# An MoE kernel on one core: dispatched rows turned by transposing DMAs in place of TensorE

## What is computed

```python
gates = softmax(x_flat @ gating_w)                   # 1024 tokens, 8 experts
topk_w, topk_idx = top_k(gates, 2)
norm_w = topk_w / sum(topk_w)
capacity = ceil(1024 * 2 / 8 * 1.25)                 # 320 slots for each expert
position = (running count of earlier picks of the same expert)
buf[expert, position] = x_flat[token]                # picks past 320 are dropped
h = relu(einsum('ecd,edh->ech', buf, w1) + b1)       # w1: 8 x 256 x 1024
out_e = einsum('ech,ehd->ecd', h, w2) + b2           # w2: 8 x 1024 x 256
out[token] += norm_w * out_e[expert, position]
```

## Time and profile before

| | us |
|---|---|
| three executions | 528.79, 537.62, 538.77 (median 537.62) |
| profiled execution | 532.26 |
| its span | 530.4 |
| TensorE busy | 453.4 |
| DVE busy | 383.9 |
| ScalarE busy | 277.2 |
| GpSimd busy | 234.2 |
| mean granted TensorE clock | 0.96 of full |

### The profile page before, as it was taken

One profiled execution on the slowest core, in us unless ns is written; L12 is line 12 of the kernel. 1 busy time (PEld: TensorE's weight loads), 2 busy tenths in 40 slices (PEclk: granted clock), 3 DMA queues, 4 the chain that ended last, 5 costly groups with the idle time before them and its releaser, 6 DMA issues. The chain is left out here.

```text
span 530.4 us, 11842 instructions
## 1 busy us (share of the span) xinstructions
PE 453.4 (85%) x4579; PEld 337.8 (64%) x4586; DVE 383.9 (72%) x873; ACT 277.2 (52%) x612; POOL 234.2 (44%) x301
## 2 busy tenths in 40 slices
PE   4964977898979999898998998897757999999984
PEld 3442544336857777787776776685534777777753
DVE  4479474767677888887886786886558588887881
ACT  2667556566355666554655454555215355556630
POOL 3275031101422222433554255433338377787764
PEclk9986699999999999999998999999978999999998
DMA  8991001930170000000060001000103666677632
GB/s 277 268 331 18 0 2 27 380 135 1 40 239 4 1 1 1 3 2 1 1 223 22 1 1 43 22 2 7 42 12 102 212 149 167 143 196 205 177 37 30
DMA packets 37720, 46.74 MB, mean 88 GB/s; under 512 B 7584, under 2 KB 33056, under 8 KB 37472
## 3 DMA queue, kind: packets, MB, share of 16 engines
q1 hardware_dynamic: 32912, 40.82, 24.1%
q0 software_dynamic: 4224, 4.79, 5.9%
q10 hardware_dynamic: 528, 0.38, 0.3%
HBM read 40.14 MB, written 8.55 MB: 92 GB/s over the span
## 5 line engine op out<-in xcount | busy, mean ns | idle before, releaser
L560 POOL TENSOR_TENSOR lw<-lw 128x512 f32<-128x512 f32 x48 | 60.7, 1269 | 113.2 <-DVE lw L1172 112.6
L868 ACT ACTIVATE lw<-psum,nmax 128x256 f32<-128x256 f32 x128 | 59.2, 469 | 19.8 <-DVE nmax L1225 19.8
L1714 PE MATMUL psum<-lp 128*128 128x256 f16 x576 | 68.4, 273 | 0.0
L1230 DVE TENSOR_TENSOR lw<-psum,lw 128x512 f16<-128x512 f32 x64 | 43.8, 684 | 28.7 <-ACT lw L875 27.7
L875 ACT ACTIVATE lw<-psum 128x512 f16<-128x512 f32 x64 | 38.2, 597 | 49.4 <-PE psum L1813 49.4
L664 POOL TENSOR_TENSOR lw<-lw 128x320 f16<-128x320 f32 x60 | 49.3, 837 | 23.0 <-DVE lw L1448 20.1
L1714 PEld LDWEIGHTS psum<-lp 128*128 128x128 f16 x576 | 54.1, 98 | 6.5 <-issue 0.5
L1976 PE MATMUL psum<-lw,se 128*128 128x320 f16 x384 | 55.2, 302 | 0.9 <-issue 0.4
L950 ACT ACTIVATE lw<-psum,b1w 128x320 f16<-128x320 f32 x64 | 33.7, 527 | 41.8 <-PE psum L1976 40.9
L1989 PE MATMUL psum<-se,lw 128*128 128x256 f16 x384 | 46.9, 281 | 7.0 <-POOL lw L664 7.0
L1813 PE MATMUL psum<-identf,lw 128*128 128x128 f32 x256 | 41.0, 283 | 13.9 <-DVE lw L1230 12.3
(11 more groups left out here) (245 smaller groups left out, 970.8 us busy)
## 6 DMA issues: line engine op xcount, KB each, us to landing
se<-in_w SPq DMA_DIRECT2D x16, 1024.0 KB, 8.0
dispatch<-in_empty SPq DMA_DIRECT2D x4, 662.5 KB, 10.1
lw<-dispatch SPq DMA_DIRECT2D x8, 265.0 KB
lp<-in_Wq SPq DMA_DIRECT2D x2, 1024.0 KB, 9.4
se<-in_WoT SPq DMA_DIRECT2D x1, 2048.0 KB, 11.8
lp<-in_w_kc_q SPq DMA_DIRECT2D x2, 768.0 KB, 9.8
x_sb<-in_x SPq DMA_DIRECT2D x2, 512.0 KB, 6.1
se<-in_gate_wT SPq DMA_DIRECT2D x1, 1024.0 KB, 9.0
```

The source lines that it names most:

```text
L560: nc.gpsimd.tensor_tensor(rope[:, c % QT, :], t1[:, c % 2, :], t2[:, c % 2, :], ALU.add)\
L868: A_(e_sb[:, n % 2, st * S:(st + 1) * S], bank[3 + n % 2][:, st * S:(st + 1) * S], ACT.Exp, bias=nmax[:, n % 2, st:st + 1], accum_out=esum ...
L1230: V.tensor_tensor(at[1][:, n % 2, :], bank[5][:, :], at[0][:, n % 2, :], ALU.subtract).then_inc(v_at, 1)
L1714: ins = M(tile_bank(c)[:, half * S:(half + 1) * S], m1[w][:, kc, half, col:col + P], (yth, ytl)[a][:, kc, b * S:(b + 1) * S], start=(n == ...
```

## The change

Rows in DRAM get 544 f16 columns (1088 bytes), so that a row starts at a multiple of 32 bytes. For experts 1 to 7 SP no longer loads whole rows: four transposing DMAs (high and low half, two blocks of 128 columns each) bring 320 rows x 128 columns each, turned, straight into one of two buffers `bufT[e % 2]`. Only the nine metadata words of a row are still loaded (three small DMAs). `turn_rows`, its copies on ScalarE and DVE and their semaphores are gone. From expert 2 on, the transposing DMAs wait until expert e-2's first product is done (`p_h`) and until all transposing DMAs of expert e-1 have landed (`d_rows`). TensorE waits for `d_rows` ahead of each expert's first product. Expert 0's rows are made as before; TensorE now waits for both halves at once (`s_bT`).

```diff
-RW = 2 * D + 2 * (1 + NE)
+META = 1 + NE
+RW = 2 * D + 32
...
-        slots_w = w3([2 * 3 * RW // 2])
+        slots_w = w3([64])[:, 0:2 * 3 * META]
...
-        bufT = w3([2, KC * CAP], F16)
+        bufT1 = w3([2, KC * CAP], F16)
+        w3([6 * 256 - KC * CAP])
+        bufT0 = w3([2, KC * CAP], F16)
+        bufT = [bufT0, bufT1]
...
                 elif e >= 2:
-                    sp.wait_ge(p_bT, 2 * (e - 1))
+                    sp.wait_ge(p_h, MH * (e - 1))
+                    sp.wait_ge(d_rows, 64 * (e - 1))
+                if e >= 1:
+                    for part in range(2):
+                        for kc in range(KC):
+                            col = part * D + kc * P
+                            sp.dma_start_transpose(bufT[e % 2][:, part, kc * CAP:(kc + 1) * CAP],
+                                                   buf_h[e * CAP:(e + 1) * CAP, col:col + P]).then_inc(d_rows, 16)
+                if e >= 2:
                     sp.wait_ge(v_meta, e - 1)
-                sp.dma_start(slots_u[:, e % 2, 0:2, :], buf_d[e * CAP:e * CAP + 2 * P, :].rearrange("(a p) c -> p a c", p=P))\
+                sp.dma_start(slots_u[:, e % 2, 0:2, :],
+                             buf_d[e * CAP:e * CAP + 2 * P, D:D + META].rearrange("(a p) c -> p a c", p=P))\
                     .then_inc(d_slot[e % 2], 16)
...
+                for j in range(2):
+                    sp.dma_start(slots_u[j * W3:(j + 1) * W3, e % 2, 2, :], buf_d[e * CAP + 2 * P:(e + 1) * CAP, D:D + META])\
+                        .then_inc(d_slot[e % 2], 16)
...
-                if e >= 1 and e + 1 < NE:
-                    rows_high(e + 1)
...
-                    rows_low(e + 1)
                     slot_meta(e + 1)
...
             for e in range(NE):
-                pe.wait_ge(a_bT, e + 1)
+                if e == 0:
+                    pe.wait_ge(s_bT, 2)
+                else:
+                    pe.wait_ge(d_rows, 64 * e)
                 pe.wait_ge(v_we, 4 * (e + 1))
...
-                                    bufT[:, a, kc * CAP:(kc + 1) * CAP], start=(k == 0), stop=(k == 5))
+                                    bufT[e % 2][:, a, kc * CAP:(kc + 1) * CAP], start=(k == 0), stop=(k == 5))
...
-                if e >= 1 and e + 1 < NE:
-                    turn_rows(e + 1)
...
-                if e == 0:
-                    turn_rows(1)
```

More of the change, by code:

```diff
@@ L207, in program @@
         w3 = carve(lw, 34)
-        slots_w = w3([2 * 3 * RW // 2])
-        slots = slots_w.bitcast(F16).rearrange("p (r i c) -> p r i c", r=2, i=3)
+        slots_w = w3([64])[:, 0:2 * 3 * META]
         slots_u = slots_w.bitcast(U32).rearrange("p (r i c) -> p r i c", r=2, i=3)
-        slots_tok = slots_u[:, :, :, D]
-        slots_wt = slots_w.rearrange("p (r i c) -> p r i c", r=2, i=3)[:, :, :, D + 1:D + 1 + NE]
-        bufT = w3([2, KC * CAP], F16)
+        slots_tok = slots_u[:, :, :, 0]
+        slots_wt = slots_w.rearrange("p (r i c) -> p r i c", r=2, i=3)[:, :, :, 1:1 + NE]
+        bufT1 = w3([2, KC * CAP], F16)
+        w3([6 * 256 - KC * CAP])
+        bufT0 = w3([2, KC * CAP], F16)
+        bufT = [bufT0, bufT1]
         hs = [w3([MH, CAP], F16) for _ in range(2)]
@@ L256, in program @@
         buf_d = nc.dram_tensor("dispatch", (SLOTS + P, RW // 2), U32).ap()
+        buf_h = buf_d.bitcast(F16)
         x_v = A["x"].rearrange("b (h p) d -> p (b h) d", p=P)
@@ L303, in program @@
         a_we, v_we = sem("a_we"), sem("v_we")
-        p_bT, a_bT, v_bT = sem("p_bT"), sem("a_bT"), sem("v_bT")
+        p_bT, s_bT, d_rows = sem("p_bT"), sem("s_bT"), sem("d_rows")
         v_hl = sem("v_hl")
@@ L427, in dispatched @@
                 elif e >= 2:
-                    sp.wait_ge(p_bT, 2 * (e - 1))
+                    sp.wait_ge(p_h, MH * (e - 1))
[7 more added lines that the diff above has]
+                if e >= 2:
                     sp.wait_ge(v_meta, e - 1)
-                sp.dma_start(slots_u[:, e % 2, 0:2, :], buf_d[e * CAP:e * CAP + 2 * P, :].rearrange("(a p) c -> p a c", p=P))\
+                sp.dma_start(slots_u[:, e % 2, 0:2, :],
+                             buf_d[e * CAP:e * CAP + 2 * P, D:D + META].rearrange("(a p) c -> p a c", p=P))\
                     .then_inc(d_slot[e % 2], 16)
-                sp.dma_start(slots_u[0:W3, e % 2, 2, :], buf_d[e * CAP + 2 * P:(e + 1) * CAP, :]).then_inc(d_slot[e % 2], 16)
-                sp.dma_start(slots_u[W3:2 * W3, e % 2, 2, D:D + 1 + NE], buf_d[e * CAP + 2 * P:(e + 1) * CAP, D:D + 1 + NE])\
-                    .then_inc(d_slot[e % 2], 16)
+                for j in range(2):
+                    sp.dma_start(slots_u[j * W3:(j + 1) * W3, e % 2, 2, :], buf_d[e * CAP + 2 * P:(e + 1) * CAP, D:D + META])\
+                        .then_inc(d_slot[e % 2], 16)
             weights(0)
@@ L931, in _ @@
             route_exp(B - 1)
[L933 to L943, removed]
+            act.wait_ge(p_bT, 1)
+            for kc in range(KC):
+                ins = A_(bufT[0][:, 0, kc * CAP:(kc + 1) * CAP], bank[SEL_BANK[0][kc]][:, 0:CAP], ACT.Copy)
+            ins.then_inc(s_bT, 1)
             for e in range(NE):
@@ L955, in _ @@
                         split_high(4 * (e + 1) + q)
-                if e == 0:
-                    rows_high(1)
         @block.vector
@@ L1420, in _ @@
             dve.wait_ge(d_b, 48)
[L1422 to L1430, removed]
+            dve.wait_ge(p_bT, 2)
+            for kc in range(KC):
+                ins = V.tensor_copy(bufT[0][:, 1, kc * CAP:(kc + 1) * CAP], bank[SEL_BANK[1][kc]][:, 0:CAP])
+            ins.then_inc(s_bT, 1)
             def slot_meta(e):
@@ L1439, in slot_meta @@
                 V.tensor_copy(tslot[:, e, 0:2], slots_tok[:, e % 2, 0:2]).then_inc(v_meta, 1)
-            rows_low(0)
             for e in range(NE):
@@ L1462, in _ @@
                     if e == 0 and i == 2:
-                        rows_low(1)
                         slot_meta(1)
@@ L1972, in _ @@
                     for a, w in PASSES:
-                        if m == 0 and a == 1:
-                            pe.wait_ge(v_bT, e + 1)
                         for kc in range(KC):
                             ins = M(bank[2 + n % 3][:, 0:CAP], we[0][w][:, e % 2, kc * EH + m * P:kc * EH + (m + 1) * P],
-                                    bufT[:, a, kc * CAP:(kc + 1) * CAP], start=(k == 0), stop=(k == 5))
+                                    bufT[e % 2][:, a, kc * CAP:(kc + 1) * CAP], start=(k == 0), stop=(k == 5))
                             k += 1
                     ins.then_inc(p_h, 1)
-                if e >= 1 and e + 1 < NE:
-                    turn_rows(e + 1)
                 if e >= 1:
```

## The result

| | before | changed |
|---|---|---|
| median of 20 runs each, us | 537.44 (525.23 to 544.46) | 543.50 (531.13 to 549.83) |
| profiled execution, us | 532.26 | 538.58 |
| its span | 530.4 | 536.8 |
| ratio | | 1.0139, 95% interval 1.0072 to 1.0207 |

The account below looks back on a forecast made before the run. Bound: TensorE's 14.8 us per expert and a nearly equal loop of landing and splitting through one raw buffer. Start gains 0.5 us, steady part nothing: 535.0 - 0.5 = 534.5 us, own range 529 to 539, widened for rivals to 526 to 560.

Parts of the forecast that it names:

- the loop of landing and splitting: Experts 3 to 6: load, landing and splits through one raw buffer take 15.42, 15.46 and 29.47 us for two; TensorE's cycle 14.8.
- the 7.8 us of turns: TensorE: six turns of 1.30 us ahead of expert 6's first product, at most 7.8 us on the path to the end.
- the 6 us forecast: Expert 1: its transposes land at 409.8, TensorE needs them at 415.77, so hidden with 6 us to spare.
- the forecast landing, 7.7 us: Expert 1's transposes: small loads end at 403.7, landing 6.1 us later at 409.8; SP's release was at 402.13.
- Rival 1: Between weight landings: transposes fill the DMA ring; 10.7 us for four gives +21 us, 555 us; chance 0.36.
- the sum: Whole kernel: 532.26 us profiled minus 0.5 gives 531.8; forecast set at 535.0 - 0.5 = 534.5 us.
- Issue 409.8 to 413.4, small loads 1.6, weights at 415.0 instead of 412.48.: SP's queue at expert 2: its transposes and small loads go first, so its weights leave at 415.0, not 412.48.
- The term of 0.9 us per transposing DMA: SP's issue time: 0.9 us each, 3.6 us for an expert's four, within a range of 1.5 to 6.6 us.
- So they are hidden and the loop stays.: Experts 3 to 6: transposes of 6.1 us fit in 7.7 us, leaving the loop at 60.35 us.
- the ring's free time: Between one expert's weights landing and the next's first byte: 5.75 us of splitting plus some 2 us, 7.7 us.
- TensorE's idle 1.5 us per expert costs clock: TensorE, expert processing: full clock expected at 13.5 of 15 us busy; if not, +2 to +8 us; chance 0.04.
- at nothing: Expert 0's start: waiting for both halves of its rows costs nothing, under 1 us exposed at worst.

## Why the prediction was wrong

Right, by its own steps: the bound was read rightly. TensorE was not alone on the path, the loop of landing and splitting was; the 7.8 us of turns brought nothing there, and the version with a second raw buffer shows them coming in once that loop is gone. The transposes stayed hidden from TensorE, with less to spare at expert 1 than the 6 us forecast: the DMA traffic of its four transposes ends at about 404.7, 7.6 us after the release, and TensorE began at 9.9. That the forecast landing, 7.7 us, fits so well is luck: the issue was taken 1.5 us too short and the rest as much too long. Rival 1's mechanism, a ring filled by movement, did not come: 2.0 us per engine, not 10.7. The median, 543.5 us, lies inside the stated range of 526 to 560, but the range was widened upwards for that rival, so this is no merit of the sum.

Wrong, and the sign with it:

1. "Issue 409.8 to 413.4, small loads 1.6, weights at 415.0 instead of 412.48." From the release that is 12.9 us; measured 17.1. The term of 0.9 us per transposing DMA was 1.25, which over the eight that stand ahead is 2.8 us. And I took the second four to start when the first had landed, at 7.7 us, and left out that SP itself was still busy: expert 1's small loads and the store of x (403.88 to 407.26) came first, so they started at 10.2 us. The landing was not the wait that ended last; SP's own list was.
2. "So they are hidden and the loop stays." I checked the transposes against the ring's free time and not against SP's. Expert 4's and expert 6's weights went out 0.9 and 0.3 us after DVE was ready, and landed 10.8 to 10.9 us after issue, against 8.1 to 9.6 us in the kernels that kept the transposes behind them. Against 9.7 that is 1.9 and 1.5 us. Why they landed later is open: the plain DMAs stood ahead of them in the same way (8.6 to 9.5 us), and so did twice the transposes (8.4 to 9.4 us).
3. The rival that "TensorE's idle 1.5 us per expert costs clock" had a chance of 0.04, since the waits were forecast even and short. They were uneven, 3.3 to 8.7 us at every second expert, and the products behind them took 1.9, 2.6 and 1.5 us more. Short waits did cost no clock, as said; the forecast of their length failed.
4. Expert 0's wait for both halves was put "at nothing". It moved DVE's splits to where less of GpSimd's work runs beside them, and expert 1 started 5.0 us earlier than before instead of the 1.3 us of its turn. Item 1 lost this again and more: expert 2 started 3.4 us later than before.

The end therefore came 11.4 us later in this pair, where the sum said 0.5 us earlier: SP's issue (items 1 and 2) made the waits, and the products behind them (item 3) took 6.0 us more than before, likely by the clock.

## What to carry to other kernels

Price an added DMA on the queue that issues it before pricing its movement, and walk the issuing engine's whole list, small loads and stores too, to where the critical transfer stands. In an in-order queue the transfer that is needed last goes last: tiny loads that an engine reads first, then the one that closes the tightest loop, then the expensive and patient ones. Work taken off the busiest engine shortens the period only when no other loop, here one raw buffer, has the same period; give that loop its second buffer first.

## What the runs showed of the hardware

- A transposing DMA of 320 x 128 two-byte elements held SP for 1.25 us (median of 28; 1.12 to 2.12), a plain one of as many bytes for 0.43 us (0.32 to 2.08); its movement took at most 0.5 us on each of the 16 engines. The Trainium skill (VectorE: DVE Perf Modes, The three transpose paths) gives 1309 ns for one block of 128 x 128. An estimate from the page's figure for four of these DMAs, ten such blocks, is 13 us; from the first issue to the end of their traffic they took some 6.0 us (398.71 to 404.7), 5.1 of them issue. The measurement decides.
- Of the first products of experts 2 to 6, those behind waits of 0.4 to 1.9 us took 6.7 to 6.9 us, as those without a wait; those behind waits of 2.2 us and more took 8.0 to 9.4 us, where the clock was read (0.77 and 0.71) a part of them at the lower level, with one exception (6.68 us behind a wait of 3.51, in the kernel where expert 0 starts early). Such a wait mostly costs 1.2 to 2.6 us beyond its own length.
- GpSimd's and DVE's instructions slow each other: eight low halves 6.0 or 10.1 us, four splits 4.6 alone and 6.6 us beside them. The Trainium skill (SBUF — State Buffer, Who interferes with whom) states that a DVE instruction with two inputs in SBUF, as the splits are, contends with a GpSimd instruction that reads SBUF, through read ports that the two share; the rows agree in kind, though no run here separates the cause.
